# The last norm, residual and store, tile by tile inside the routed stage

## The chip, the cores and the metric

The kernel runs on one core of a Trainium2 chip. A core has five engines with instruction queues of their own: TensorE (PE, matrix products into PSUM), VectorE (DVE), ScalarE (ACT), GpSimd (POOL) and SyncE (SP, which here only issues DMAs). They work side by side and wait for one another through semaphores. The metric is the device time of one execution in microseconds. The kernel before takes 1456.02 us, the median of 3 runs (1454.44 to 1457.98).

## The reference

Input x is 8 sequences of 512 tokens with 256 features in float32. Two sublayers, each with a layer norm in front and one behind:

```
x = x + layernorm(mamba(layernorm(x)))
x = x + layernorm(ffn(layernorm(x)))
```

`mamba` is an input projection, a convolution over 4 tokens, a scan over 512 time steps with 16 states for each of 512 channels, and an output projection. `ffn` is a mixture of experts with one shared expert:

```
score  = sigmoid(max(x @ gate_w));  expert = argmax(x @ gate_w)       # 8 experts
routed = swiglu(x * score) with the weights of the token's one expert
shared = swiglu(x) with the shared weights
ffn    = shared + routed
```

A layer norm here is (v - mean) / sqrt(var + 1e-5) over the 256 features.

## The kernel before

**Scan stage.** The sequences go one after the other through a pipeline of 32 quarter steps each (`iteration`). Beside the scan the kernel writes to DRAM, for each sequence, the rows after the first sublayer (`x1_rows`, the later residual) and their normalized form (`xn_rows`, and transposed `xn_columns`). SP also fills `slot_in` with zeros once, early (line 418). The shared expert's result for sequence 0 is made within this stage.

**Shared stage.** TensorE runs the shared expert over the other 7 sequences. ScalarE copies the result out of PSUM into `ysh`, which stays in SBUF for all tokens (`sh_keep`, L908). Beside it VectorE works out the routing: each token gets a slot number so that the tokens of an expert stand together and each expert's slots fill whole tiles of 128; with 4096 tokens and 8 experts that makes 39 tiles, some slots empty. GpSimd multiplies the normalized rows by the score and scatters them to `slot_in` by indirect DMA, 32 tiles of 128 tokens (L574, L580). SP loads the expert weights.

**Routed stage.** Slot tiles s = 0 to 38, each of one expert. In `step(s)` TensorE issues: the transposes of the slot rows of tile s+2 (`xsT_`, L1632, into bank psB), the transposes of the activation of tile s (`actT_`, L1650), the gate and up projections of tile s+1 (`up_`, L1641), and the down projection of tile s (`down_`, L1658). VectorE copies xsT (L1264) and actT (L1276) out of PSUM and multiplies silu(gate) by up (`rt_act`, actN, L1270); ScalarE makes the silu (L949), copies the down projection out of PSUM (`rt_out`, L955) and stores it to `slot_out` (L957). SP reloads one of two slot buffers as soon as its transposes are made (L452). Each engine's order is written out by hand; these loops are loops of the machine (`Fori`), two tiles a round. GpSimd has nothing to do.

**Last stage.** It begins when all 39 tiles are stored. GpSimd gathers the routed rows back in token order, 32 indirect DMAs into a ring of eight pairs `fy` (L591). For each pair of token tiles VectorE adds `ysh` (`fin_sum`, L1302) and takes the statistics (L1305, L1310), ScalarE works out 1/sqrt by Ln and Exp and normalizes (`fin`, L980 to L991), VectorE adds the residual (`fin_out`, L1316; the residual rows were loaded into `fx0` and `fx1`), and SP stores to the result.

Of the kernel before, what the change touches and what calls it, by code (L numbers as in the profile page):

```python
# [7 lines left out]
F32 = mybir.dt.float32  # L8
# [5 lines left out]
P = 128  # L14
# [5 lines left out]
def build(nc, x, winT, conv_w, xprojT, dt_w, dt_b, A_log, D, woutT, norm_w, norm_b,  # L20
# [32 lines left out]
    FRING = 8  # L53
# [5 lines left out]
    xs_d = nc.dram_tensor("slot_in", (SLOT_TILES * P, DIM), F32).ap()  # L59
    y_d = nc.dram_tensor("slot_out", (SLOT_TILES * P, DIM), F32).ap()  # L60
    bc_d = nc.dram_tensor("bc_rows", (NB, 2 * N, L), F32).ap()
    ysh_d = nc.dram_tensor("shared_rows", (P, J, DIM), F32).ap()

    ctx = ExitStack()
    with ctx:
# [73 lines left out]

        fst = [sb(f"fst{i}", [P, 2, 6], where=M) for i in range(FRING)]  # L140
        fmv = [sb(f"fmv{i}", [P, 2, 2], where=M) for i in range(FRING)]
        fln = [sb(f"fln{i}", [P, 2], where=M) for i in range(FRING)]
        fnm = [sb(f"fnm{i}", [P, 2], where=M) for i in range(FRING)]
        frs = [sb(f"frs{i}", [P, 2], where=M) for i in range(FRING)]
        actT = [sb(f"actT{i}", [P, FC, P], where=M) for i in range(2)]
        yo = [sb(f"yo{i}", [P, DIM], where=M) for i in range(2)]
        sb("xg_rest", [P, 2 * KC * L - FRING * 22 - 2 * FC * P - 2 * DIM], where=M)
        WG = ExitStack()
        ctx.enter_context(WG)
        wg = sb("wg", [P, E, KC, FF], where=WG)  # L150
        WG.close()

        HALF = NT // 2
        fx1 = sb("fx1", [P, HALF, DIM], where=M)
        sb("wg_rest", [P, E * KC * FF - HALF * DIM], where=M)
        wu = sb("wu", [P, E, KC, FF], where=M)
        wd = sb("wd", [P, E, FC, DIM], where=M)
        fx0 = sb("fx0", [P, HALF, DIM], where=M)
        ysh = sb("ysh", [P, NT, DIM], where=M)
        sg = [sb(f"sg{i}", [P, FF], where=M) for i in range(2)]  # L160
        xsl = [sb(f"xsl{i}", [P, DIM], where=M) for i in range(2)]
# [7 lines left out]
        fy = [sb(f"fy{i}", [P, 2, DIM], where=M) for i in range(FRING)]  # L169
# [23 lines left out]
        xrow = [fx0[:, i * J:(i + 1) * J] for i in range(2)]  # L193
# [35 lines left out]
        ysh_loaded = sem("ysh_loaded")  # L229
# [77 lines left out]
        yo_ready = sem("yo_ready")  # L307
        yo_stored = [sem(f"yo_stored{i}") for i in range(2)]
        gathered = [sem(f"gathered{i}") for i in range(FRING)]
        f_loaded = [sem(f"f_half_loaded{i}") for i in range(2)]  # L310
        f_chain = sem("final_chain")
        f_normed = sem("final_normed")
        f_mv = sem("final_mv")
        f_rs = sem("final_rs")
        f_ready = sem("final_ready")
        f_stored = [sem(f"f_stored{i}") for i in range(2)]
# [5 lines left out]
        x1t_v = x1_d.rearrange("(t p) c -> p t c", p=P)  # L322
        xst_v = xs_d.rearrange("(t p) c -> t p c", p=P)
        yt_v = y_d.rearrange("(t p) c -> t p c", p=P)
        outp_v = out.rearrange("b (q h p) c -> (b q) p h c", p=P, h=2)
# [9 lines left out]
        def _(sp):  # L335
# [44 lines left out]
            def iteration(i, par, do_lead, do_front, do_scan, do_back):  # L380
# [8 lines left out]
                if do_back and not (do_scan or do_front):  # L389
                    sp.wait_ge(summed, NB * Q)  # L390
                    for k in range(2):
                        sp.dma_start(xrow[k], xnb_v[k]).then_inc(xrow_loaded[k], 16)
# [21 lines left out]
                if do_front:  # L414
# [5 lines left out]
                         ao[:, 0:1].broadcast_to([P, SLOT_TILES, DIM])).then_inc(slots_zeroed, 16)  # L420
# [10 lines left out]
            for i in range(2):  # L431
# [3 lines left out]
            sp.dma_start(ysh_d.rearrange("p j d -> p (j d)"),  # L435
                         tmp[:, 0:2].rearrange("p h t -> p (h t)")).then_inc(e_stored, 16)
# [13 lines left out]
            for b in range(2, NB):  # L450
                sp.wait_ge(scattered[b % 2], 16 * J * (b // 2))
                sp.dma_start(xrow[b % 2], xnb_v[b]).then_inc(xrow_loaded[b % 2], 16)  # L452
# [11 lines left out]
            def load_residual(dst, h):  # L464
                for g in range(NB // 2):
                    rows = slice((h * NB // 2 + g) * J, (h * NB // 2 + g + 1) * J)
                    sp.dma_start(dst[:, g * J:(g + 1) * J, :], x1t_v[:, rows, :]).then_inc(f_loaded[h], 16)

            sp.wait_ge(e_stored, 16)
            sp.dma_start(ysh[:, 0:J, :], ysh_d).then_inc(ysh_loaded, 16)  # L470
            load_residual(fx0, 0)
            with sp.Fori(0, SLOT_TILES - 4, 2) as s:
                for i in range(2):
                    sp.wait_ge(xsT_ready, s + i + 1)
                    load_slots(s + i + 2, i)
            for s in range(SLOT_TILES - 3, SLOT_TILES - 2):
                sp.wait_ge(xsT_ready, s + 1)
                load_slots(s + 2, s % 2)


            sp.wait_ge(r_up, SLOT_TILES)
            load_residual(fx1, 1)

            def store_out(q, i, src, first):
                sp.wait_ge(f_ready, q + 1)
                sp.dma_start(outp_v[bass.ds(q, 1)].rearrange("a p h c -> p (a h) c"),
                             src[:, bass.ds(2 * (q - first), 2), :]).then_inc(f_stored[i], 16)

            NQ = NT // 2
            for h, src in enumerate((fx0, fx1)):  # L490
                with sp.Fori(h * NQ // 2, (h + 1) * NQ // 2 - 1, 2) as q:
                    for i in range(2):
                        store_out(q + i, i, src, h * NQ // 2)
            sp.wait_ge(f_stored[0], 16 * (NQ // 2))
# [1240 lines left out]
```

## Time and profile before

| | us |
|---|---|
| median of 3 runs | 1456.02 |
| profiled execution, its time | 1456.55 |
| profiled execution, its span in the trace | 1454.6 |
| TensorE busy | 1180.4 (81%) |
| VectorE busy | 1029.7 (71%) |
| GpSimd busy | 997.9 (69%) |
| ScalarE busy | 801.9 (55%) |

The busy times are averages over stages with different limits: in the scan stage GpSimd and VectorE are busy almost throughout, in the shared and routed stages TensorE. The page also gives the granted clock of TensorE, in shares of full speed, and for each group of instructions the idle time of its engine just ahead of it with what ended that. Idle time of an engine that isn't the limit costs nothing. GpSimd's line L591 is an example of how to read this: it shows 286.6 us of idle time before it, 277.2 of them ended by the store of `slot_out`, which means only that GpSimd had no work during the routed stage.

### The profile page before, as it was taken

What the parts mean: (1) busy time and instruction counts of PE and PEld (TensorE: products, weight loads), DVE (VectorE), ACT (ScalarE), POOL (GpSimd) and SP (SyncE); (2) the same over time, 40 slices, a digit from 0 to 9 for tenths busy, and PEclk for the clock granted to TensorE, in tenths of its full rate; (3) what the DMA queues carried; (4) which work ended last, traced back from release to release, by engine and by line L of the source; (5) the groups of instructions that cost most, each with busy time, mean ns of one, the idle gap of its engine ahead of it and who ended that gap; (6) DMA issues with size and microseconds to landing.
All of it is one profiled execution on the core that took longest, in us unless ns stands there. A gap on an engine that the chain in (4) does not pass through costs nothing.

```text
span 1454.6 us, 15610 instructions
## 1 busy us (share of the span) xinstructions
PE 1180.4 (81%) x4782; PEld 521.0 (36%) x4783; DVE 1029.7 (71%) x1067; ACT 801.9 (55%) x1388; POOL 997.9 (69%) x468
## 2 busy tenths in 40 slices
PE   5667768878887896986987878889999999999930
PEld 2221223223222331421422322334566566666620
DVE  3598999999999989999999897993411122222237
ACT  5757458667677776875866865654411111111137
POOL 0589999999999999999999999993137000000035
PEclk9898899899899899999989999999999999999975
DMA  3901211230240250141122024002584211111145
GB/s 104 330 1 59 88 58 41 95 113 31 73 145 3 74 174 0 61 152 37 60 87 87 31 73 173 0 15 93 198 316 147 88 37 43 43 43 43 40 130 174
DMA packets 78246, 129.56 MB, mean 89 GB/s; under 512 B 7649, under 2 KB 56417, under 8 KB 74081
## 3 DMA queue, kind: packets, MB, share of 16 engines
q1 hardware_dynamic: 68768, 112.60, 23.1%
q0 software_dynamic: 3072, 8.39, 1.8%
q10 hardware_dynamic: 6336, 7.74, 1.5%
q8 instruction: 33, 0.54, 0.2%
q14 instruction: 37, 0.30, 0.1%
HBM read 96.46 MB, written 32.24 MB: 88 GB/s over the span
## 4 chain that ended last, share of the span: by engine, by line
PE 35%; POOL 33%; issue 15%; DVE 10%; ACT 6%; DMA 1%; POOLq 0%; ACTq 0%; SPq 0%; DVEq 0%
POOL state L528 20%; PE psX L1641 10%; POOL bx L517 10%; PE psX L1576 6%; DVE state L1111 6%; PE psY L1589 3%; PE bank L1658 2%; PE psY L1658 2%; POOL fy L591 2%; PE bank L1445 2%; POOL lt L533 2%; PE psY L1523 2%; ACT psX L754 1%; DVE bx L1099 1%; PE psY L1650 1%
## 5 line engine op out<-in xcount | busy, mean ns | idle before, releaser
L528 POOL TENSOR_TENSOR state<-state,cbc 128x1024 f32<-128x1024 f32 x256 | 605.6, 2388 | 16.1 <-DVE state L1111 16.0
L1111 DVE TENSOR_TENSOR_SCAN state<-psX,bx 128x1024 f32<-128x1024 f32 x256 | 578.5, 2279 | 38.7 <-ACT psX L754 22.3
L754 ACT ACTIVATE psX<-dt,aneg 128x511 f32<-128x511 f32 x512 | 330.6, 679 | 198.8 <-DVE state L1111 197.2
L517 POOL TENSOR_TENSOR bx<-xh,bbc 128x1024 f32<-128x1024 f32 x120 | 290.0, 2417 | 59.5 <-DMA bbc<-bc_rows 43.1
L1523 PE MATMUL psY<-state,ident 64*64 64x512 f32 x2048 | 288.0, 656 | 16.9 <-POOL state L528 16.8
L1480 PE MATMUL bank<-prow,ident 128*128 128x512 f32 x272 | 171.8, 717 | 112.9 <-DVE bx L1099 112.9
L591 POOL DMA_INDIRECT fy<-slot_out,slot x32 | 33.5, 1047 | 286.6 <-DMA slot_out<-yo 277.2
L1099 DVE TENSOR_TENSOR bx<-xh,bank 128x1024 f32<-128x1024 f32 x136 | 162.6, 1195 | 8.6 <-PE bank L1480 8.5
L1523 PEld LDWEIGHTS psY<-state,ident 64*64 64x64 f32 x2048 | 64.4, 140 | 202.7 <-issue 127.6
L1270 DVE TENSOR_TENSOR actN<-sg,psX 128x512 f32<-128x512 f32 x39 | 26.8, 687 | 141.1 <-ACT sg L949 141.1
L1480 PEld LDWEIGHTS bank<-prow,ident 128*128 128x128 f32 x272 | 48.5, 212 | 207.1 <-DVE bx L1099 166.7
L949 ACT ACTIVATE sg<-psX 128x512 f32<-128x512 f32 x39 | 23.3, 597 | 155.3 <-PE psX L1641 155.3
L1188 DVE TENSOR_TENSOR actS<-sg,psX 128x512 f32<-128x512 f32 x28 | 19.0, 685 | 102.8 <-ACT sg L902 102.8
L1641 PE MATMUL psX<-wg,xsT 128*128 x156 | 77.2, 617 | 1.1 <-DVE xsT L1264 0.6
L1641 PE MATMUL psX<-wu,xsT 128*128 x156 | 73.3, 592 | 0.0
L1400 PE MATMUL bank<-lt,win 128*128 128x512 f32 x112 | 55.6, 618 | 17.9 <-DVE acc L1046 16.5
L574 POOL TENSOR_TENSOR fx<-fx,score 128x1024 f32<-128x1024 f32 x8 | 15.3, 1911 | 74.0 <-DVE slot L1251 54.7
L1046 DVE SCALAR_TENSOR_TENSOR acc<-bank,cw,acc 128x511 f32<-128x511 f32 (+2 forms) x84 | 62.3, 741 | 3.9 <-ACT acc L645 1.9
L1445 PE MATMUL bank<-wout,yv 128*128 128x256 f32 x256 | 58.5, 382 | 1.7 <-ACT yv L700 1.6
L902 ACT ACTIVATE sg<-psX 128x512 f32<-128x512 f32 x28 | 16.6, 596 | 76.8 <-PE psX L1576 76.7
L1576 PE MATMUL psX<-xg,shg 128*128 128x512 f32 x112 | 53.1, 596 | 1.6 <-DVE actS L1188 1.6
L1445 PEld LDWEIGHTS bank<-wout,yv 128*128 128x128 f32 x256 | 48.0, 190 | 17.3 <-issue 9.0
(190 smaller groups left out, 1579.6 us busy)
## 6 DMA issues: line engine op xcount, KB each, us to landing
cbc<-bc_rows SPq DMA_DIRECT2D x32, 1024.0 KB, 5.0
bbc<-bc_rows SPq DMA_DIRECT2D x16, 1024.0 KB, 6.1
slot_in<-ao SPq DMA_DIRECT2D x1, 4992.0 KB, 27.9
xsl<-slot_in SPq DMA_DIRECT2D x39, 128.0 KB, 2.2
slot_out<-yo ACTq DMA_DIRECT2D x39, 128.0 KB, 2.4
xin<-in_x SPq DMA_DIRECT2D x8, 512.0 KB, 4.3
xr<-in_x SPq DMA_DIRECT2D x8, 512.0 KB, 5.4
x_rows<-ao SPq DMA_DIRECT2D x8, 512.0 KB, 2.9
```

Of the source, the lines that this page charges most:

```text
L517: nc.gpsimd.tensor_tensor(bx[q % RB][:], xh[par][:, h * CH:(h + 1) * CH], bbc[:, n // 2].unsqueeze(1).broadcast_to([P, CH, L]), ALU.mult). ...
L528: nc.gpsimd.tensor_tensor(w[:], w[:], cbc[:, n].unsqueeze(1).broadcast_to([P, CH, L]), ALU.mult).then_inc(weighted, 1)
L591: nc.gpsimd.indirect_dma_start(out=fy[q % FRING][:, t % 2, :], out_offset=None, in_=y_d, in_offset=bass.IndirectOffsetOnAxis(slot[:, t:t + ...
L754: e = nc.scalar.activation(decay[q % RD][:, c, 1:L], dt[par][:, h * CH + c, 1:L], ACT.Exp, scale=aneg[:, h * CH + c, n:n + 1])
L1046: last = nc.vector.scalar_tensor_tensor(out=acc[:, c, m:L], in0=psF[:, 0:L - m], scalar=cw[:, c, TAPS - 1 - m:TAPS - m], in1=acc[:, c, m:L ...
L1099: nc.vector.tensor_tensor(bx[q % RB][:], xh[par][:, h * CH:(h + 1) * CH], psB[:].unsqueeze(1).broadcast_to([P, CH, L]), ALU.mult).then_inc ...
L1111: nc.vector.tensor_tensor_scan(st[q % RS][:].rearrange("p c t -> p (c t)"), decay[q % RD].rearrange("p c t -> p (c t)"), bx[q % RB][:].rea ...
L1445: last = nc.tensor.matmul(psF[:, (j % 2) * DIM:(j % 2 + 1) * DIM], yv[:, c, j * P:(j + 1) * P], wout[:, c], start=(c == 0), stop=(c == C - 1))
L1480: nc.tensor.matmul(psB[:], ident[:, n:n + 1].broadcast_to([P, P]), prow[par][:], start=True, stop=True).then_inc(b_bcast, 1)
L1523: done = nc.tensor.matmul(psY[o * HP:(o + 1) * HP, r], weights(half, c), src[half, c], start=first, stop=last_)
L1576: last = nc.tensor.matmul(bank, w[:, k, c * P:(c + 1) * P], xg[g % 2][:, k], start=(k == 0), stop=(k == KC - 1))
L1641: last = nc.tensor.matmul(bank, xsT[i][:, k], w[:, bass.ds(ereg[i], 1), k].rearrange("p a n -> p (a n)"), start=(k == 0), stop=(k == KC - 1))
```

## The change

The token order is given up for the end of the kernel: each routed tile is finished where it stands. A slot row carries a 257th number, from which the token's number is read; empty slots carry 0, which gives 4096 and is out of bounds, so that the indirect DMAs leave such rows out. For tile s

- VectorE makes the index from the slot row (`token_index`);
- GpSimd gathers the shared rows (`ysl`, ring of 4) and the residual rows (`x1l`, ring of 8) of these tokens (`get`), and six tiles later scatters the finished tile to the result (`put`);
- VectorE adds the down projection, straight from PSUM, to the shared rows (`rt_sum`, one tile behind) and takes the statistics; for each pair of tiles it works out 1/sqrt with a bit trick and three Newton steps, in two halves (`root_begin`, `root_end`);
- ScalarE normalizes a pair (`rt_norm`), and VectorE adds the residual (`rt_add`).

The shared rows are therefore stored to DRAM, sequence by sequence, from ScalarE's queue. The loops of the routed stage on VectorE, ScalarE and GpSimd are now written out; TensorE's stay as they were. `slot_out`, the second table load, the residual loads and the old last stage are gone.

```diff
-    FRING = 8
+    YR = 8
+    SR = 4
+    IR = 16
+    PUT_LAG = 6
...
-    xs_d = nc.dram_tensor("slot_in", (SLOT_TILES * P, DIM), F32).ap()
-    y_d = nc.dram_tensor("slot_out", (SLOT_TILES * P, DIM), F32).ap()
+    xs_d = nc.dram_tensor("slot_in", (SLOT_TILES * P, DIM + 1), F32).ap()
...
@@ SP @@
                 for i in range(2):
                     sp.wait_ge(xsT_ready, s + i + 1)
+                    sp.wait_ge(idx_ready, s + i + 1)
                     load_slots(s + i + 2, i)
...
-            sp.wait_ge(r_up, SLOT_TILES)
-            load_residual(fx1, 1)
...
@@ GpSimd @@
+                nc.gpsimd.tensor_copy(xrow[b % 2][:, :, DIM:DIM + 1],
+                                      ids[:, b * J:(b + 1) * J].unsqueeze(2)).then_inc(xrow_scaled, 1)
...
+            def get(s):
+                pool.wait_ge(idx_ready, s + 1)
+                if s >= SR:
+                    pool.wait_ge(y_summed, s - SR + 1)
+                nc.gpsimd.indirect_dma_start(out=ysl[:, s % SR, :], out_offset=None, in_=ysh_d, in_offset=by_token(s),
+                                             bounds_check=TOK - 1, oob_is_err=False).then_inc(ysl_loaded[s % SR], 16)
+                if s >= YR:
+                    pool.wait_ge(o_ready, s - YR + 1)
+                nc.gpsimd.indirect_dma_start(out=x1l[:, s % YR, :], out_offset=None, in_=x1_d, in_offset=by_token(s),
+                                             bounds_check=TOK - 1, oob_is_err=False).then_inc(x1l_loaded[s % YR], 16)
+
+            def put(s):
+                pool.wait_ge(o_ready, s + 1)
+                nc.gpsimd.indirect_dma_start(out=out_v, out_offset=by_token(s), in_=yo[s % YR][:], in_offset=None,
+                                             bounds_check=TOK - 1, oob_is_err=False).then_inc(out_stored[s % YR], 16)
+
+            pool.wait_ge(s_down, 2 * LATE)
+            nc.gpsimd.memset(ysl[:], 0.0).then_inc(rings_zeroed, 1)
+            nc.gpsimd.memset(x1l[:], 0.0).then_inc(rings_zeroed, 1)
+            pool.wait_ge(rings_zeroed, 2)
+            pool.wait_ge(ysh_stored, 16 * LATE)
...
+            for s in range(SLOT_TILES + PUT_LAG):
+                if s < SLOT_TILES:
+                    get(s)
+                if s >= PUT_LAG:
+                    put(s - PUT_LAG)
@@ ScalarE @@
+                act.wait_ge(s_kept, 2 * g + 2)
+                act.dma_start(yshb_v[LATE_FROM + g],
+                              ysh[:, (LATE_FROM + g) * J:(LATE_FROM + g + 1) * J, :]).then_inc(ysh_stored, 16)
...
+            def rt_norm(k):
+                act.wait_ge(ln_ready, k + 1)
+                for s in range(2 * k, min(2 * k + 2, SLOT_TILES)):
+                    nc.scalar.activation(yo[s % YR][:], yo[s % YR][:], ACT.Identity,
+                                         scale=frs[k % 2][:, s % 2:s % 2 + 1],
+                                         bias=fnm[k % 2][:, s % 2:s % 2 + 1]).then_inc(y_normed, 1)
...
+            for s in range(SLOT_TILES):
+                rt_silu(s, s % 2)
+                if s >= 4 and s % 2 == 0:
+                    rt_norm(s // 2 - 2)
@@ VectorE @@
+            def rt_sum(s):
+                dve.wait_ge(r_down, s + 1)
+                dve.wait_ge(ysl_loaded[s % SR], 16 * (s // SR + 1))
+                if s >= YR:
+                    dve.wait_ge(out_stored[s % YR], 16 * (s // YR))
+                nc.vector.tensor_tensor(yo[s % YR][:], (psF, psG)[s % 2][:, 0:DIM], ysl[:, s % SR, :],
+                                        ALU.add).then_inc(y_summed, 1)
+                dve.wait_ge(y_summed, s + 1)
+                linked(nc.vector.bn_stats(out=fst[s % 2][:], in_=yo[s % YR][:]))
+                nc.vector.memset(carrier[:], 0.0)
+                linked(nc.vector.bn_aggr(out=fmv[s // 2 % 2][:, s % 2, :], in_=fst[s % 2][:]))
+
+            def newton(k, w):
+                y, v, q = part(frs, k, w), part(fvar, k, w), part(fsq, k, w)
+                linked(nc.vector.scalar_tensor_tensor(out=q, in0=y, scalar=-0.5, in1=y, op0=ALU.mult, op1=ALU.mult))
+                linked(nc.vector.tensor_tensor(q, q, v, ALU.mult))
+                linked(nc.vector.scalar_tensor_tensor(out=y, in0=q, scalar=1.5, in1=y, op0=ALU.add, op1=ALU.mult))
...
+            for s in range(SLOT_TILES):
+                if s + 2 < SLOT_TILES:
+                    copy_xsT(s + 2, s % 2)
+                    token_index(s + 2)
+                copy_actT(s, s % 2)
+                if s >= 1:
+                    rt_sum(s - 1)
+                if s % 2 == 0 and s >= 2:
+                    root_begin(s // 2 - 1)
+                if s % 2 == 1 and s >= 3:
+                    root_end(s // 2 - 1)
+                if s % 2 == 0 and s >= 4:
+                    rt_add(s - 4)
+                    rt_add(s - 3)
+                if s + 1 < SLOT_TILES:
+                    rt_act(s + 1, (s + 1) % 2)
+            T = SLOT_TILES
+            root_end(T // 2 - 1)
+            rt_sum(T - 1)
+            root_begin(T // 2, 1)
+            root_end(T // 2, 1)
+            for s in range(T - 3, T):
+                rt_add(s)
@@ TensorE, down_ @@
-                    pe.wait_ge(yo_ready, s - 1)
+                    pe.wait_ge(y_summed, s - 1)
```

`linked` adds one to a semaphore at an instruction's end and makes the next instruction of VectorE wait for it.

The next rows show VectorE in one round of the routed loop of the kernel before, two steps: xsT is the transposed slot rows, actT the transposed activation, actN the activation.

```order
L1264 COPY xsT<-bank 128x256
L1275 REGISTER_ALU
L1276 COPY actT<-psY 128x512
L1267 REGISTER_ALU
L1270 TENSOR_TENSOR actN<-sg,psX 128x512
L1261 REGISTER_ALU
L1264 COPY xsT<-bank 128x256
L1276 COPY actT<-psY 128x512
L1270 TENSOR_TENSOR actN<-sg,psX 128x512
```

In the changed kernel the same engine has this between the actT copy and actN of an even step (here s = 36; yo is the tile's row ring, ysl the shared rows, fvar to fsq the root's small tiles, x1l the residual rows):

```order
L1273 TENSOR_TENSOR yo<-psY,ysl 128x256
L1276 BN_STATS fst<-yo 128x6
L1277 MEMSET carrier 128x1
L1278 BN_AGGR fmv<-fst 128x2
L1291 TENSOR_SCALAR fvar<-fmv 128x2
L1292 TENSOR_SCALAR fbit<-fvar 128x2
L1293 TENSOR_SCALAR frs<-fbit 128x2
L1285 SCALAR_TENSOR_TENSOR fsq<-frs 128x2
L1286 TENSOR_TENSOR fsq<-fsq,fvar 128x2
L1287 SCALAR_TENSOR_TENSOR frs<-fsq,frs 128x2
L1306 TENSOR_TENSOR yo<-yo,x1l 128x256 x2
L1249 TENSOR_TENSOR actN<-sg,psX 128x512
```

Twelve instructions now stand between the copy and the multiplication that TensorE waits for, where there was none.

GpSimd before, from the last scatters of slot rows on (fx holds the scaled rows):

```order
L574 TENSOR_TENSOR fx<-fx,score 128x1024
L580 DMA slot_in<-fx,slot 4992x256 x4
L574 TENSOR_TENSOR fx<-fx,score 128x1024
L580 DMA slot_in<-fx,slot 4992x256 x4
L591 DMA fy<-slot_out,slot 128x256 x32
```

GpSimd in the changed kernel, the last two rounds of the routed stage (result is the output, x_rows the residual rows):

```order
L581 DMA ysl<-shared_rows,idx 128x256
L585 DMA x1l<-x_rows,idx 128x256
L590 DMA result<-yo,idx 4096x256
L581 DMA ysl<-shared_rows,idx 128x256
L585 DMA x1l<-x_rows,idx 128x256
L590 DMA result<-yo,idx 4096x256 x7
```

The 32 gathers in one run are gone; each tile has two gathers and a scatter, and seven scatters stand at the end.

## Rows read from the trace of the kernel before

**Rows 1.** windows view of two stretches: length, busy us by engine, PEclk, DMA share, GB/s
```profile
1157.00:1396.70 239.70, 236.54 (x854) 142.84 (x854) 69.37 (x115) 38.20 (x78) 0.00 (x0) 1.00 0.16 46
1396.70:1454.60 57.90, 0.00 (x0) 0.00 (x0) 36.16 (x112) 35.91 (x114) 33.50 (x32) 0.53 0.53 164
```

**Rows 2.** waits of the routed stage: engine, line waited for, us, times, longest
```profile
ACT sg L949 <- PE psX L1641: 155.3, 39, 5.3
```

**Rows 3.** chain that ended last, in order of time: start, us, what
```profile
1157.11 3.71 PE psX L1641 x8
...
1387.59 3.69 PE psX L1641 x8
...
1394.32 2.00 PE bank L1658 x8
...
1396.76 4.62 DMA slot_out<-yo
...
1440.70 4.03 DMA fy<-slot_out,slot
...
1451.09 0.69 DVE fx L1316
```

**Rows 4.** timeline of one routed step, all engines: start, us, engine, line, operation, idle before
```profile
1300.40 0.60 ACT L949 ACTIVATE sg<-psX 128x512 f32<-128x512 f32 x1 [4.00 <-PE psX L1641]
...
1301.03 0.69 DVE L1270 TENSOR_TENSOR actN<-sg,psX 128x512 f32<-128x512 f32 x1 [3.58 <-ACT sg L949]
...
1302.14 0.60 PE L1650 MATMUL psY<-ident,actN 128*128 128x128 f32 x4
...
1302.34 0.42 DVE L1264 COPY xsT<-bank 128x256 f32<-128x256 f32 x1 [0.63 <-PE bank L1632]
...
1302.78 0.69 DVE L1276 COPY actT<-psY 128x512 f32<-128x512 f32 x1
```

**Rows 5.** timeline of VectorE in the routing chain
```profile
1045.20 0.42 DVE L1238 TENSOR_TENSOR q<-bank,incl 128x256 f32<-128x256 f32 x1
...
1046.12 0.17 DVE L1242 TENSOR_SCALAR ti<-incl 128x8 int32<-128x8 f32 x1
...
1046.33 0.17 DVE L1243 TENSOR_SCALAR ti<-ti 128x8 int32<-128x8 int32 x1
```

**Rows 6.** the stretch after the routed stage, by line and form: busy us, mean ns
```profile
L591 POOL DMA_INDIRECT fy<-slot_out,slot x32 | 33.5, 1047 | 286.6 <-DMA slot_out<-yo 277.2 <-issue 9.4
...
L991 ACT ACTIVATE fy<-fy,fnm,frs 128x256 f32<-128x256 f32 x32 | 17.5, 592 | 0.5
...
L1305 DVE BATCH_NORM_STATS2 fst<-fy 128x6 f32<-128x256 f32 x32 | 12.0, 418 | 0.5
...
L1310 DVE BATCH_NORM_AGGREGATE fmv<-fst 128x2 f32<-128x6 f32 x32 | 3.9, 163 | 0.7
```

**Rows 7.** timelines of GpSimd and VectorE in the last stage
```profile
1418.34 1.35 POOL L591 DMA_INDIRECT fy<-slot_out,slot  x1 [0.31 <-issue]
...
1419.07 0.69 DVE L1302 TENSOR_TENSOR fy<-fy,ysh 128x512 f32<-128x512 f32 x1 [0.21 <-DMA fy<-slot_out,slot]
```

**Rows 8.** end of the scatter on GpSimd and of the shared stage
```profile
1123.49 0.96 POOL L580 DMA_INDIRECT slot_in<-fx,slot  x1 [0.30 <-issue]
...
1155.06 0.38 PE L1632 MATMUL bank<-ident,xsl 128*128 128x128 f32 x2
...
1155.26 0.60 ACT L908 ACTIVATE ysh<-psY 128x512 f32<-128x512 f32 x1 [2.86 <-PE psY L1589]
```

**Rows 9.** DMA issues of the whole program: KB each, median us to landing
```profile
slot_in<-ao SPq DMA_DIRECT2D x1, 4992.0 KB, 27.9
...
slot_in<-fx,slot POOLq DMA_INDIRECT x32, 3.5
```

**Rows 10.** start of the program, timelines of the SP queue and of GpSimd
```profile
41.58 0.57 SPq L419 DMA_DIRECT2D slot_in<-ao  x1
...
107.06 4.68 POOL L528 TENSOR_TENSOR state<-state,cbc 128x1024 f32<-128x1024 f32 x2
```

## What is predicted

> **What bounds the kernel now.** I read the windows first, to cut the span where the kernel's stages end, then the chain that ended last, then the waits and one step's timeline. The routed stage (39 tiles of 128 slots) is TensorE's: it is busy 236.54 of 239.70 us at granted clock 1.00, that is 2.4 GHz, while VectorE is busy 69 us and GpSimd not at all; in the 57.90 us behind it TensorE does nothing [rows 1]. ScalarE's silu waits 155.3 us for TensorE there, 39 times [rows 2]. The chain gives the pace: from the first tile's up-projection at 1157.11 to the last one's at 1387.59 are 38 steps, 6.065 us each. The last down-projection ends at 1396.32. Then a store has to land, all 32 gathers go through GpSimd one behind the other, and the last add runs from 1451.09 to 1451.78 [rows 3]; the span ends at 1454.60, 2.82 us later, with the last store. So 58.3 us stand behind TensorE's end, and the change can win at most these. It can lose wherever a step comes to need more than 6.065 us.
>
> **The slack in a step.** In one step [rows 4] silu ends, VectorE multiplies (actN) from 1301.03 to 1301.72, and TensorE's four transposes of it start at 1302.14: actN could be about 0.4 us later before TensorE waits. The copy of these transposes (actT) runs from 1302.78 to 1303.47, and VectorE then idles 3.58 us until the next actN. The window for new work between copy and actN is thus 3.58 + 0.4 = 3.98 us. Into it go, for every tile, the sum with the shared part and its statistics, and by turns the first or the second half of the root and the two residual adds.
>
> **Prices on VectorE.** The sum (128x256, one operand in PSUM): 0.42 [rows 5]. Statistics 0.42, aggregate 0.16 [rows 6], the small memset in its shadow. Each instruction that waits for its forerunner starts about 0.04 late: the two dependent 128x8 instructions start 0.21 apart with 0.17 of work [rows 5]. So sum and statistics are 0.46 + 0.46 + 0.20 = 1.12 us. A link of the root's chain (128x2) is taken as 0.21. The trace shows no such Newton step; it is bounded by 0.17 without a wait and by 0.46, what a dependent 128x256 instruction takes; I take 0.21, the row nearest in size. The residual add is 0.42, from the sum's row again; a 128x512 add is 0.69 [rows 7], so it lies between 0.35 and 0.69.
>
> Even step: 1.12 + 6 links 1.26 + 2 adds 0.84 = 3.22 us. The token index (128x1, 0.17 or less) stands ahead of the actT copy and delays it by at most 0.1, since the copy would start only 0.02 after the xsT copy. 3.22 + 0.1 against 3.98 leaves 0.66 us. Odd step: 1.12 + 7 links 1.47 = 2.59, leaving 1.3. I cost the whole new VectorE work of the stage at nothing: TensorE's up-projection and silu cover it. If the cover is gone, each of the 17 even steps with adds (s = 4 to 36) pays its overrun in full. With both bounds put in, an even step is 1.12 + 1.02 + 0.70 = 2.84 or 1.12 + 2.76 + 1.38 = 5.26: from nothing to an overrun of 1.4 us, or 24 us in all.
>
> **ScalarE.** The two normalizations of a pair (0.59 each, rows 6) follow an even step's silu, which ends 1301.00 in rows 4, so they end about 1.2 us later and the adds that wait for them come 4 us later; the next silu is 6 us off. The copy out of PSUM and 39 stores leave ScalarE, and TensorE's down-projection waits for VectorE's sum two tiles back, a step before it. Nothing.
>
> **GpSimd and the queues.** Three indirect DMAs per tile. In the last stage one takes 1.047 on average and 0.30 between two [rows 6, 7], the longest shown 1.35 + 0.31. Three are 4.0 us, at worst 5.0, of 6.065. The gather of shared rows for tile s may be issued in step s-2, and its sum stands in step s+1; residual rows have longer, and a scatter is six tiles behind its gather. What queues behind a waiting scatter are the next gathers, which have two steps to spare. The bound check on the index, and the rows that it drops, are in no row: from below such a DMA is as short as an undisturbed one, 0.96 [rows 8]; from above I put GpSimd's 128x1024 multiply, 4.68 / 2 = 2.34 [rows 10], and three of these are 7.0 a tile, 0.95 over the step or 36 us in all. I take the gather's own row, nothing lost, and leave the upper end to a rival.
>
> The stage's start: the last shared rows are copied at 1155.86 [rows 8]. Two memsets of 3072 columns are less than three such multiplies, 7.0 us, so the gathers start between 1159 and 1163, and the first sum is due after the actT copy of tile 1, two steps behind 1157.11, near 1170; a landing takes 3.5 us [rows 9]. Covered.
>
> Ahead of the stage: the seven 512 KB stores and eight tiny copies lie beside the shared stage. GpSimd's scatter ends 1124.45 and the first slot transpose is at 1155.06 [rows 8], 30 us of cover. SP's slot loads now also wait for the index, about 0.5 us later, with a whole step of slack; SP loses the residual loads. The slot fill, now 1028 bytes a row, goes out at 41.58 and lands 27.9 later [rows 9, 10], at 69.5. The C rows queued behind it are read from 107 on, so it may even double. Nothing.
>
> **The new tail**, from the old clock. TensorE ends at 1396.32. VectorE has had the last actT copy at 1394.2: sum of tile 37 to 1395.4, first half of root 18 to 1396.6, two adds to 1397.5, second half to 1398.9, sum of tile 38 to 1400.1, both halves of root 19 (13 links) to 1402.8, with the normalization of tile 38 to 1403.5 and its add to 1403.9. Tiles 36 and 37 are added from 1402.8 on; GpSimd scatters three tiles from 1403.3, the third at 1403.3 + 2 x 1.27 = 1405.8 (1.27 where it is undisturbed, 0.96 + 0.30, rows 8), landing 3.5 later at 1409.3 [rows 9], and about 0.5 to the end of the span, my share of the 2.82 above, which hold a store's landing and the end. Span 1409.8. Gain: 58.3 - 13.5 = 44.8 us. The profiled execution took 1456.55 for its span of 1454.60, 1.95 more, and lies 0.53 above the median of 1456.02. 1409.8 + 1.95 - 0.53 = 1411.2 us, so 1411.
>
> **Rivals.**
> *The window overruns* (0.14). An instruction with two or three waits may cost more than the 0.04 seen. For it: eleven of the even step's twelve instructions behind the copy wait, and the spare is 0.66 us. Against it: the dependent instructions of the routing chain keep 0.21. With 0.1 more for eleven it pays (1.1 - 0.66) x 17 = 7 us; with the upper bound 24. I take 13, toward the middle: 1424.
>
> *The shared port* (0.11). In rows 7 a GpSimd DMA runs from 1418.34 to 1419.69 and a VectorE add with both operands in SBUF starts at 1419.07 inside it and takes its plain 0.69, so VectorE isn't held; GpSimd's DMA is 0.4 longer than the undisturbed. If VectorE were held for the DMAs that fall into its window, an even window of 3.2 us would meet 6 x 3.2 / 12.13 = 1.6 of them, 1.5 us, 0.8 over the spare, in 17 steps 14 us: 1425. The Trainium skill speaks against this change here: "SBUF — State Buffer", section "Who interferes with whom", has VectorE and GpSimd share one port pair as an exclusive lock, for which a VectorE instruction with two SBUF inputs or in a two-port mode contends, and the later one blocks. By that rule the time is 1425; the trace agrees for GpSimd's side alone.
>
> *GpSimd becomes the bound* (0.09), the one that ends on the other side. Mechanism: a bound-checked indirect DMA costs more than the gather in the rows, or small VectorE instructions hold it up. From 2.02 us each (6.065 / 3) it sets the pace of the routed stage; from 2.02 + 44.8 / 114 = 2.41 us the kernel is slower than before. At 2.5 it is 7.5 x 38 - 230.5 = +54 us: 1466. For it: 117 of them inside the stage, where before there was none, and the price of the bound check is unknown. Against: 1.66 is the longest distance seen with VectorE as busy.
>
> *Early work isn't covered* (0.06): the 1028-byte rows triple the fill, or the weight and slot traffic delays the first tile: some 9 us, 1420.
>
> **How the numbers follow.** Forecast 1411 with 0.60; its own range is 1405 to 1418 (tail links at 0.17, scatters landing in 3; or a first step late by some us). A difference under 0.2% (3 us) can't be told from none. Of GpSimd's 0.09, 0.06 end slower, 0.01 the same and 0.02 faster. So faster 0.93, same 0.01, slower 0.06. The range runs from 1405 to 1432: it takes in the window and port cases but for the last of their upper bound, and leaves out GpSimd's.
>
> **What would show it.** Right: TensorE's step stays 6.07 at clock 1.00; VectorE's idle time before actN is 0.3 to 0.5 in even steps and near 1 in odd ones; 117 indirect DMAs near 1.0 to 1.35; some 13.5 us from TensorE's end to the span's end. Wrong: TensorE's transposes waiting for actN, with even steps longer than odd ones (window, or port, if the wait falls on GpSimd's DMAs); sums waiting for shared rows and GpSimd without idle time (GpSimd bound); a first tile later than 1157 (early work).

## The result, and the profile after

The changed kernel takes 1411.37 us (median of 4 runs, 1410.87 to 1412.14), the kernel before 1455.23 beside it (1454.25 to 1457.98): a ratio of 0.9699, 95% interval 0.968 to 0.9718. Forecast were 1411. The profiled execution took 1411.09 us for a span of 1409.3.

The same two stretches as in [rows 1], in the windows view of the changed kernel:

```profile
1157.00:1396.70 239.70, 236.49 (x854) 142.59 (x853) 159.53 (x579) 40.88 (x75) 115.36 (x113) 1.00 0.25 75
1396.70:1409.30 12.60, 0.00 (x0) 0.00 (x0) 5.64 (x29) 1.69 (x3) 4.92 (x5) 0.60 0.02 2
```

TensorE's stage is as it was, to 0.05 us, and at the same clock (1.00, that is 2.4 GHz). VectorE does 90 us more beside it and GpSimd 115 us where it did nothing, and the stretch behind has shrunk from 57.90 to 12.60 us. The chain that ended last, in order of time, against [rows 3]:

```profile
1156.74 3.71 PE psX L1647 x8
...
1387.59 3.69 PE psX L1647 x8
...
1394.09 0.42 DVE yo L1273
...
1402.25 0.84 DVE yo L1306 x2
...
1405.72 0.98 POOL result L590
```

38 steps from 1156.74 to 1387.59 are 6.075 us each (6.065 before). Where the old chain went on with a store, gathers and a last add at 1451, it now leaves TensorE for VectorE's sums, roots and adds, and ends with a scatter on GpSimd. TensorE's last product ends at 1396.31, and 13.0 us stand behind it, where the forecast had 13.5. Who waits in the routed stage (engine, line waited for, us, times, longest), against [rows 2]:

```profile
ACT sg L961 <- PE psX L1647: 196.5, 39, 5.6
POOL ysl L581 <- DVE idx L1258: 75.9, 36, 3.9
...
DVE actN L1249 <- ACT sg L961: 41.6, 38, 4.5
...
PE psY L1656 <- DVE actN L1249: 1.2, 1, 1.2
```

GpSimd waits 76 us for token indices: it has time. TensorE's transposes wait for an actN once (1.2 us); in the kernel before this wait is there too (1.3 us, once). One even step with its adds, from the timeline, against [rows 4]:

```profile
1294.75 0.69 DVE L1249 TENSOR_TENSOR actN<-sg,psX 128x512 f32<-128x512 f32 x1 [1.17 <-ACT sg L961]
...
1296.50 0.69 DVE L1255 COPY actT<-psY 128x512 f32<-128x512 f32 x1
1297.11 0.42 DVE L1273 TENSOR_TENSOR yo<-psY,ysl 128x256 f32<-128x256 f32 x1
...
1298.66 1.01 POOL L585 DMA_INDIRECT x1l<-x_rows,idx  x1 [0.31 <-issue]
1298.90 0.16 DVE L1285 SCALAR_TENSOR_TENSOR fsq<-frs 128x2 f32<-128x2 f32 x1
1299.09 0.16 DVE L1286 TENSOR_TENSOR fsq<-fsq,fvar 128x2 f32<-128x2 f32 x1
...
1299.48 0.76 DVE L1306 TENSOR_TENSOR yo<-yo,x1l 128x256 f32<-128x256 f32 x2
1300.20 0.60 ACT L961 ACTIVATE sg<-psX 128x512 f32<-128x512 f32 x1 [4.51 <-PE psX L1647]
...
1300.84 0.69 DVE L1249 TENSOR_TENSOR actN<-sg,psX 128x512 f32<-128x512 f32 x1 [0.59 <-ACT sg L961]
```

Links of the root's chain start 0.19 to 0.20 apart. The new work, sum to last add, runs from 1297.11 to 1300.24, 3.13 us. VectorE then idles 0.59 us before actN in this even step and 1.17 in the odd one (the first row). GpSimd's DMAs in the same stretch, by line and form, against [rows 6]:

```profile
L581 POOL DMA_INDIRECT ysl<-shared_rows,idx x39 | 40.3, 1033 | 80.6 <-DVE idx L1258 75.9 <-issue 4.7
L585 POOL DMA_INDIRECT x1l<-x_rows,idx x39 | 39.2, 1006 | 11.9 <-issue 11.9
...
L590 POOL DMA_INDIRECT result<-yo,idx x34 | 35.2, 1036 | 23.3 <-DVE yo L1306 18.1 <-issue 5.2
```

They take 1.01 to 1.04 us with the bound check, where the unchecked gathers took 1.047. And the issues of the whole program, against [rows 9]:

```profile
slot_in<-ao SPq DMA_DIRECT2D x1, 5011.5 KB, 35.1
...
result<-yo,idx POOLq DMA_INDIRECT x39, 2.5
```

Last the end, in the timeline:

```profile
1397.64 0.98 POOL L590 DMA_INDIRECT result<-yo,idx  x1 [9.39 <-DVE yo L1306]
...
1398.46 1.09 ACT L966 ACTIVATE yo<-yo,fnm,frs 128x256 f32<-128x256 f32 x2 [5.57 <-DVE fnm L1300]
...
1400.38 0.99 POOL L590 DMA_INDIRECT result<-yo,idx  x1 [1.76 <-issue]
...
1401.91 1.17 DVE L1306 TENSOR_TENSOR yo<-yo,x1l 128x256 f32<-128x256 f32 x3
...
1403.14 0.98 POOL L590 DMA_INDIRECT result<-yo,idx  x1 [1.77 <-DVE yo L1306]
...
1405.72 0.98 POOL L590 DMA_INDIRECT result<-yo,idx  x1 [0.30 <-issue]
```

The rows of tiles 36 and 37 are normalized by 1399.55 and wait for their add until 1401.91, behind the root of tile 38. From the last scatter's start to the end are 3.6 us. What they hold is seen only at the line to which the engines' closing drains are put down (operation, duration ns, start):

```profile
L68 POOLq DRAIN  x1: 5050/5050/5050, 1404.0 to 1404.0; - x1
...
L68 SPq DRAIN  x1: 13/13/13, 1408.1 to 1408.1; - x1
```

SP, which waits for all scatters to land, is done at 1408.1; GpSimd's drain runs to 1409.07, and this is what ends the program. Its record begins at 1404.0, before the last two scatters, so its 5.05 us cover these and their landing as well; 0.9 us of it stands behind SP.

### The profile page after: what moved, and what is told of

Read it like the earlier page. It is cut to its first block, busy times and chain, and to the rows that moved or that the text cites. A ratio compares the mean times of both kernels' runs of the same rounds, so it can differ in the third digit from the quotient of the medians.

```text
span 1409.3 us, 15754 instructions
## 1 busy us (share of the span) xinstructions
PE 1175.4 (83%) x4782; PEld 518.5 (37%) x4783; DVE 1089.8 (77%) x1449; ACT 770.9 (55%) x1275; POOL 1088.4 (77%) x565
## 4 chain that ended last, share of the span: by engine, by line
PE 36%; POOL 29%; issue 15%; DVE 12%; ACT 8%; DMA 0%; POOLq 0%; ACTq 0%; SPq 0%; DVEq 0%
POOL state L511 18%; PE psX L1647 10%; POOL bx L500 9%; DVE state L1090 6%; PE psX L1582 5%; PE psY L1595 3%; PE psY L1664 2%; PE bank L1664 2%; PE psY L1529 2%; PE bank L1451 2%; POOL lt L516 2%; ACT psX L763 2%; PE bank L1486 1%; DVE bx L1078 1%; DVE acc L1025 1%
## 5 line engine op out<-in xcount | busy, mean ns | idle before, releaser
L581 POOL DMA_INDIRECT ysl<-shared_rows,idx x39 | 40.3, 1033 | 80.6 <-DVE idx L1258 75.9
L1406 PE MATMUL bank<-lt,win 128*128 128x512 f32 x112 | 55.5, 618 | 15.7 <-DVE acc L1025 14.4
L590 POOL DMA_INDIRECT result<-yo,idx x39 | 40.1, 1029 | 36.8 <-DVE yo L1306 29.3
L1249 DVE TENSOR_TENSOR actN<-sg,psX 128x512 f32<-128x512 f32 x39 | 26.8, 688 | 44.1 <-ACT sg L961 41.6
## 6 DMA issues: line engine op xcount, KB each, us to landing
slot_in<-ao SPq DMA_DIRECT2D x1, 5011.5 KB, 35.1
```

## The experiments

All of them change the changed kernel, but for one, and keep its computation unless it is said. The kernel before took 1455.2 to 1456.1 us beside them, and 1464.6 beside the three runs told of where they stand.

**Is VectorE's window as wide as I took it?** Added links in every even step that has adds, ahead of actN (a product of 128x2 whose result nobody reads):

```diff
...
                     rt_add(s - 4)
                     rt_add(s - 3)
+                    if s + 1 < SLOT_TILES:
+                        for _ in range(4):
+                            linked(nc.vector.tensor_tensor(fdum[:], fvar[0][:], fvar[0][:], ALU.mult))
```

> Four more dependent 128x2 multiplications on VectorE in each of the 17 even steps that have residual adds, between the adds and actN (their result isn't used). In the changed kernel's trace a link takes 0.195 us, so 0.78 us more per even step. Theory W (the window): VectorE idles 0.59 us before actN in such a step, and actN may be 0.4 us late before TensorE's transposes wait, so 0.95 us are to spare; nothing is paid: 1411 us. Rival F (no slack behind actN: what delays it is paid in full): 0.78 - 0.55 = 0.2 us in 17 steps, 1415 us.

> Eight such links in each of the 17 even steps, 1.56 us more. Theory W: 0.6 us over the spare of 0.95 us, paid 17 times, 10 us: 1422 us, with TensorE's transposes waiting for actN in even steps alone. Rival F: 1.0 us in 17 steps, 1428 us. If VectorE's delay were caught up again in the odd steps, which have 1.2 us idle, it would be 1411 us.

Measured: four links 1413.35 us (1412.55 to 1414.46; ratio 0.9715, 0.9684 to 0.9746), eight 1427.46 (1426.42 to 1429.47; 0.9817, 0.9786 to 0.9849). With four, actN starts 0.1 to 0.2 us behind silu's end in most of these steps (0.03 in the changed kernel), and the stage is 2.3 us longer (38 steps in 233.19 instead of 230.85, 0.14 for each of the 17 even ones), so even that little isn't absorbed. With eight, actN starts 0.91 to 0.97 us behind silu's end in most of them, and the 38 steps take 246.54 us, 15.7 more, or 0.92 for each even one: TensorE pays all of it. The 0.4 us between actN and the transposes were no slack. TensorE's waits with eight links, and its timeline, say why:

```profile
PE psY L1660 <- DVE actN L1250: 7.5, 17, 1.2
PE psX L1651 <- issue: 5.0, 16, 0.3
```

```profile
1296.12 0.69 DVE L1250 TENSOR_TENSOR actN<-sg,psX 128x512 f32<-128x512 f32 x1
...
1296.87 0.66 PE L1660 MATMUL psY<-ident,actN 128*128 128x128 f32 x4 [0.35 <-DVE actN L1250]
...
1297.82 1.98 PE L1651 MATMUL psX<-wg,xsT 128*128 x4 [0.30 <-issue]
```

The wait for actN is 0.35 to 0.4 a time, as the 0.4 of slack would have it; but then TensorE loses another 0.3 waiting for nothing that the profile shows, and starts its next product 0.95 us after the transposes instead of 0.62. At line 1676 of this kernel, just behind the wait for actN, its sequencer reads the next tile's expert number: a load of 0.30 us and about 0.2 of register work. With the order turned round:

```diff
...
                 if ahead:
                     xsT_(s + 2, i)
+                if more:
+                    expert(s + 1, 1 - i)
                 actT_(s, i)
                 if more:
-                    expert(s + 1, 1 - i)
                     up_(s + 1, 1 - i)
```

> The eight added links of the run before, and one thing moved: TensorE's sequencer reads the number of the next tile's expert (a load of 0.30 us, then 0.15 and 0.02 us of register work) ahead of its wait for actN, not behind it. In the run with eight links actN is ready 0.91 us late in every even step, and the step is 0.87 longer; the first matmul of the next product starts 0.95 us after the transposes of actN, against 0.62 in the changed kernel, with 0.3 us put down to issue (17 times, 5.3 us in all). Theory R (the lost 0.3 us is the sequencer's: its load waits behind the late actN, and only there): with the load ahead of the wait the first matmul starts 0.62 to 0.7 after the transposes, an even step is 6.6 to 6.65, the stage gives back 17 x 0.3 = 5 us, and the time is 1422 to 1423. Rival X (it is VectorE's: the copy of xsT stands behind the late actN and comes late too): nothing moves, even steps stay at 6.94, 1427.

Measured: 1417.26 us (1417.0 to 1419.29), beside a kernel before of 1464.59 (ratio 0.9679, 0.9664 to 0.9694). The times of two chips are hard to set against each other, so I go by the profiles: 38 steps take 235.81 us (first product at 1159.74, last at 1395.55) instead of 246.54. The load was the lost time, but it was worth 10.7 us, twice what I expected of it, since it was not paid in the late steps alone. With the load first, from the timelines of VectorE and TensorE, a late actN and one that isn't late; then TensorE in an undisturbed step of the changed kernel:

```profile
1294.07 0.69 DVE L1250 TENSOR_TENSOR actN<-sg,psX 128x512 f32<-128x512 f32 x1
...
1295.30 1.88 PE L1651 MATMUL psX<-wg,xsT 128*128 x4
...
1299.57 0.69 DVE L1250 TENSOR_TENSOR actN<-sg,psX 128x512 f32<-128x512 f32 x1 [0.94 <-ACT sg L962]
...
1300.68 0.60 PE L1660 MATMUL psY<-ident,actN 128*128 128x128 f32 x4
...
1301.12 1.88 PE L1651 MATMUL psX<-wg,xsT 128*128 x4
...
1302.84 1.88 PE L1651 MATMUL psX<-wu,xsT 128*128 x4
```

```profile
1295.87 0.60 PE L1656 MATMUL psY<-ident,actN 128*128 128x128 f32 x4
...
1296.47 1.98 PE L1647 MATMUL psX<-wg,xsT 128*128 x4
...
1298.29 1.88 PE L1647 MATMUL psX<-wu,xsT 128*128 x4
```

From transposes to product 0.44 instead of 0.60, and the product's first half 1.72 instead of 1.82: about 0.26 us in every step. The pace of 6.07 us that I had taken for TensorE's own work, in both kernels, has the sequencer's load in it.

The distance from the end of actN to TensorE's next product says it most plainly. With the load behind the wait it is 1.03 us where actN isn't late (1295.44 to 1296.47 in the changed kernel) and 1.01 where it is late by 0.9 (1296.81 to 1297.82), so all lateness is passed on. With the load first it is 0.86 where actN isn't late (1300.26 to 1301.12) and 0.54 where it is (1294.76 to 1295.30): 0.3 us of lateness is absorbed, and the slack that I had read is there once nothing of the sequencer stands behind the wait.

How the changed kernel does with the load first and no added links wasn't run; 38 x 0.26 is 9.9 us, as an estimate, if VectorE's even steps (0.59 us idle) follow.

**How near is GpSimd to being the bound?** One and three more gathers per tile, of shared rows into a ring that nobody reads:

```diff
...
+                if s < SLOT_TILES:
+                    for j in range(3):
+                        more(3 * s + j)
```

> One more gather of 128 shared rows per tile on GpSimd, into a spare ring that nothing reads, 39 more in all: four indirect DMAs per tile. Theory G (GpSimd's cost is its issue time, 1.03 + 0.30 us each, beside everything): 4 x 1.33 = 5.3 us of a step's 6.07, nothing is paid: 1411 us. Rival P (GpSimd's DMAs hold up VectorE through a shared port): one more in every step, up to 1 us in the even step's window against a spare of 0.95 us: 1411 to 1415 us, with VectorE's instructions longer or later in the window.

> Three more gathers per tile, six indirect DMAs in all. Theory G: 6 x 1.33 = 8.0 us per tile, 1.9 over the step of 6.07 in 38 steps: about 1411 + 73 = 1484 us, slower than the kernel before, with GpSimd without idle time in the routed stage and the sums waiting for it. Rival: if the DMAs' issue overlaps (the 0.30 us between them vanishes when they are queued, or one waits only for its descriptors), 6 x 1.0 = 6.0 and the time stays near 1411.

Measured: one more, 1415.15 us (1414.76 to 1415.65; ratio 0.9727, 0.9697 to 0.9757); three more, 1482.24 (1479.48 to 1483.3; 1.0185, 1.0151 to 1.0219). One more leaves the step at 6.073 us and VectorE's idle time before actN at 42.3 us (41.6 in the changed kernel), so the 4 us that it costs aren't the port rival's; 3.6 of them stand behind TensorE's end (see the next experiment). Three more make GpSimd the bound, as my third rival had it, and the kernel slower than before. In VectorE's waits, 1160 to 1450, and in GpSimd's timeline:

```profile
DVE yo L1287 <- DMA ysl<-shared_rows,idx: 82.4, 29, 3.4
```

```profile
1384.29 1.01 POOL L585 DMA_INDIRECT ysl<-shared_rows,idx  x1 [0.30 <-issue]
...
1392.24 1.01 POOL L585 DMA_INDIRECT ysl<-shared_rows,idx  x1 [0.30 <-issue]
```

Six DMAs take 7.95 us, 1.325 each with the 0.30 between them, and the sums wait for shared rows. The changed kernel's three take 3.97 of 6.075.

**Do GpSimd's DMAs hold VectorE up?** Both gathers left out, so that zeros are added for the shared part and for the residual:

```diff
...
-                if s < SLOT_TILES:
-                    get(s)
...
```

> Leaves out both gathers of each tile (78 indirect DMAs): the shared and residual rows added are zeros from the rings' memset. The scatters stay. Theory W/G (TensorE sets the pace, GpSimd's DMAs are hidden and hold nobody up): 1411 us within 0.2%, VectorE's instructions in an even step as long as in the changed kernel. Rival P (the DMAs hold VectorE up through a shared port, hidden by its spare): time 1411 us too, but VectorE's idle time before actN in even steps grows from 0.59 us by a good part of a DMA's 1.03 us. Rival D (traffic or late rows cost the step's pace its last hundredth, 6.075 against 6.065 us): 0.4 us less.

Measured: 1415.54 us (1414.3 to 1416.39; ratio 0.9723, 0.9707 to 0.9739), not faster at all. The step stays at 6.07 us, and VectorE's idle time before actN is what it was (41.6 with the gathers):

```profile
DVE actN L1248 <- ACT sg L960: 42.8, 38, 4.5
```

So the gathers cost VectorE about 1 us over 39 tiles, and TensorE nothing. The span of this profile is 5.3 us longer than the changed kernel's. TensorE's first product began 2.1 us later, already behind a slower scan; the stage was 0.3 shorter; and 3.5 are at the other end, as in the run with one gather more. There GpSimd's closing drain is 3.4 to 3.6 us longer:

```profile
L68 POOLq DRAIN  x1: 8445/8445/8445, 1405.9 to 1405.9; - x1
...
L68 SPq DRAIN  x1: 13/13/13, 1409.9 to 1409.9; - x1
```

SP has seen everything land by 1409.9, and the span ends at 1414.6. With one gather more the two numbers are 8.64 us and 1409.0. The record of a drain can begin before the last scatters, so its length isn't a price; the time from the last scatter's start to the end of the span is. That is 3.58 us, to 0.01, in the changed kernel (both times), with links, with extra fills and with either other tail, nine profiles in all, and 7.1 and 7.2 in these two and 9.5 with three more gathers. In just these three there is no pause between the first two scatters of the end (0.30 us), where each of the nine has one of 1.75 or 1.76. What joins the two stays open; it isn't the number of DMAs, since one of the two has more and one fewer.

**What would halving the old gathers have given?** The kernel before with 16 of its 32 gathers (the other rows are zeros):

```diff
...
-            for t in range(NT):
+            for t in range(0, NT, 2):
...
```

> The kernel before, with only the first of each pair's two gathers (16 instead of 32; the other half of each pair is zero rows plus the shared rows). It asks what bound the old last stage. Theory G (GpSimd's 32 DMAs, 1.35 us apart, 43 of its 58 us): with one per pair the next limit is ScalarE's chain of about 2.3 us per pair, 16 x 2.3 = 36 after the first: the stage gets about 5 to 8 us shorter, 1448 to 1451 us. Rival (a gather's bandwidth or landing bound it, or ScalarE and VectorE did already): no change, 1455 us. If GpSimd alone had bound it, it would fall by 21 us to 1434.

Measured: 1447.45 us (1439.1 to 1447.81; ratio 0.993, 0.9904 to 0.9957), 8.7 us less. GpSimd was the old tail's bound by that much only: behind it ScalarE and VectorE are busy 34.6 and 34.9 of the 48.9 us left, and GpSimd's last gathers each wait 1.10 us for VectorE. The 44 us came from putting the whole tail beside TensorE, not from cheaper gathers.

**Is the slot fill free, and why is it slower?** First the fill three times over, and the scatter made to wait for all:

> The zero fill of the slot rows is made three times (two of them into spare tensors, ahead of the real one): some 35 us each. The prediction gave it cover until the C rows behind it are read at 107 us: three fills end near 42 + 105 = 147. Theory C (cover to 107, then paid in full, as the queue is in order): 107 to about 147, some 30 to 45 us lost: 1441 to 1456. Rival (the later loads share the engines and aren't behind the fill, or the scan has slack of its own): 1411 to 1420.

Measured: 1430.18 us (1424.4 to 1431.19; ratio 0.9829, 0.9812 to 0.9845), between the two expectations; the wait is another one (VectorE, 30 to 170 us):

```profile
DVE bst L1009 <- DMA xin<-in_x: 18.5, 1, 18.5
```

Not the C rows are late but the next block's input tile, issued behind the fills. In the changed kernel it lands at 78.3 and is first read at 98.98, 20.7 us of room. That is what is left after the fill had grown by 7.2: in the kernel before the tile lands at 70.8 and is read from 98.4 on, 27.6 us of room. So "may even double" (27.9 more) named about the whole of it, though from another limit, the C rows at 107. Two more fills move the tile's landing by 37 us and not by 70: they overlap, and the three land at 74.2, 93.6 and 114.4. Then four extra fills of one size, well apart, in iterations 1 to 4, that differ in the floats of a row and the distance between rows:

```diff
+    FORMS = ((257, 257), (257, 320), (256, 256), (256, 257))
```

> Four more fills of 4992 rows into spare tensors, one behind each of the iterations 1 to 4, from a constant tile: rows of 1028 bytes at a pitch of 1028; 1028 at 1280; 1024 at 1024; 1024 at 1028. It asks why the slot fill went from 27.9 to 35.1 us. Only the time from issue to landing of each counts; the whole time is longer. Theory A (the start's alignment in DRAM costs it): slow, fast, fast, slow, near 35 and 28. Theory L (the length, one more piece of 4 bytes): slow, slow, fast, fast. Both: the second and fourth between.

Measured: 1412.28 us (one run), and landings of 27.6, 23.6, 21.0 and 28.0 us, in this order. Rows of 257 floats at a distance of 320 take 2.6 more than the plain form, either kind of row at a distance of 257 about 7 more. That is the size of the 7.2 us between [rows 9] and 35.1. With one measurement for each form, it is mainly the distance between the rows that costs (the second and fourth forms tell it from the length); why, and how much of the 2.6 is the longer row, isn't shown.

**Can the end be shorter?** The adds of tiles 36 and 37 ahead of the last root; and, in a second kernel, two Newton steps in place of three besides:

```diff
...
+            rt_add(T - 3)
+            rt_add(T - 2)
             root_begin(T // 2, 1)
             root_end(T // 2, 1)
-            for s in range(T - 3, T):
-                rt_add(s)
+            rt_add(T - 1)
```

> The changed kernel with the last adds of tiles 36 and 37 ahead of the last root and not behind it. In the changed kernel their rows are ready (ScalarE's norm ends 1399.55) 2.4 us before they are added (1401.91). Now they are added from 1399.5 to 1400.35, root 19 and its norm come 0.84 later, its add ends at 1403.9 against 1403.08, and by 0.8 us from the end of an add to its scatter (1402.34 to 1403.14) the last scatter starts at 1404.7 against 1405.72, where it stood third in a row of 1.29 each. Theory Q (the end is set by three scatters in a row behind one add): the end is 1.0 us earlier, 1410.4. Rival Z (GpSimd's pause of 1.76 us between two scatters comes again, or the three scatters still meet): 1411.0 to 1411.7, no change.

> As the run with the last adds moved, and with two Newton steps for each root and not three (less exact, by design): three links less in every odd step and in each of the two roots of the end. In the stage nothing changes (odd steps already have time to spare: TensorE's step stays 6.07). At the end the links are on the path: root 18 and root 19 are 3 x 0.195 = 0.58 us shorter each, so that the last add is 1.17 us earlier. Theory Q: 1410.4 - 1.2 = 1409.2. Rival Z: scatters of 36 and 37 hold the last one back (each takes 1.29): 1410.0 or more.

Measured, beside a kernel before of 1464.59: 1410.0 us (1408.89 to 1411.96; ratio 0.963, 0.9617 to 0.9643) and 1409.72 (1408.4 to 1411.57; 0.9631, 0.9618 to 0.9644). To have the changed kernel's own spread beside them:

> The changed kernel itself, unaltered, once more, since the two runs with another tail were timed on a chip on which the kernel before took 1464.6 us, and the changed kernel's own 1411.4 stands beside 1455.2. Theory Q (the tail runs gained what their profiles show behind TensorE's end: 11.8 and 11.5 us against 13.0): the changed kernel takes 1411 to 1412, 1.2 to 1.7 us more than they did, and 13.0 us stand behind TensorE's end again. Rival: the chips differ by more than that for this kernel too, in which case its time is outside 1410.5 to 1412.5 and the gain of the tail runs can be read from their profiles alone.

Measured: 1412.43 us (1410.95 to 1413.08), but beside 1455.27 (ratio 0.9702, 0.9689 to 0.9716), so on another chip again. The ratios can't be compared, and by the times the gain of 1.4 to 2.7 us is about what can be told. The profiles have it from the start of TensorE's last product: the changed kernel ends 14.98 us later (the same when run again), with the adds moved 13.81, with two Newton steps as well 13.49. The first gain is 1.2 us, where 1.0 was expected; of the second, 1.2 expected, only 0.3 came. The timeline with both:

```profile
1399.38 0.98 POOL L590 DMA_INDIRECT result<-yo,idx  x1 [1.76 <-DVE yo L1305]
...
1401.21 0.43 DVE L1305 TENSOR_TENSOR yo<-yo,x1l 128x256 f32<-128x256 f32 x1 [0.67 <-ACT yo L966]
1401.94 0.98 POOL L590 DMA_INDIRECT result<-yo,idx  x1 [0.30 <-DVE yo L1305]
1403.23 0.98 POOL L590 DMA_INDIRECT result<-yo,idx  x1 [0.30 <-issue]
```

The last add is done at 1401.64 and its scatter starts at 1403.23, behind the one before it: the pause of 1.76 us ahead of it in this row of scatters, which is in the changed kernel as well, leaves no room for the rest. In all of these kernels the span ends 3.58 us behind the last scatter's start.

## Why the prediction was right, and where it wasn't

**The step.** Right: 6.075 us at clock 1.00, VectorE's idle time 0.59 and 1.17 (forecast 0.3 to 0.5 and near 1), the new work hidden. Links cost 0.195 instead of 0.21, and the even step 3.13 instead of 3.22. The step of the argument that failed is "actN could be about 0.4 us later before TensorE waits": the runs with added links show that TensorE pays for a lateness of less than 0.2 already (2.3 us over the stage), since a load of its sequencer stands behind the wait; with the load moved ahead of it, 0.3 us is absorbed. The spare was the 0.59 us of idle time and no more. For an even step heavier by 0.6 to 1.0 us the same reasoning would have forecast no loss, and been wrong.

**GpSimd.** Right: 3.97 us a tile, the bound check costs nothing that shows (1.01 to 1.04 us against 1.047), and at twice the number it is the bound, slower than before.

**The port.** The rival is refuted, by the run without gathers. The residual adds have both operands in SBUF; the pair at 1299.48 begins inside a GpSimd DMA (1298.66 to 1299.67) and takes 0.38 an add. All that the trace shows is some 0.04 us on a small instruction under which a DMA starts: the root's third link takes 0.213 us (median of 18), and 0.169 in the run without gathers, where none starts there. The Trainium skill's rule ("SBUF — State Buffer", section "Who interferes with whom"), as I applied it in the prediction, would have held these adds up, and the trace disagrees. I had left out a line of the same section: two inputs in SBUF contend with a GpSimd instruction that reads SBUF, and it infers that a tensor_tensor doesn't stall the issue of DMAs. With that the trace agrees: the adds take their 0.38 us inside a DMA.

**Early work.** Right that it is covered; the fill was mis-sized, 35.1 us for 27.9. What it must not delay is the next input tile at 98.98, not the C rows at 107; behind the longer fill 20.7 us of room are left. The scatter of slots ended at 1128.55, 4.1 later than before, and was covered.

**The end.** The steps hold: scatters forecast from 1403.3 and the third at 1405.8, measured 1403.14 and 1405.72. The last term, landing and end, was put at 4.0 us and measured 3.6, but it is another one than I named: these scatters land in 2.1, and GpSimd's drain ends the program. A size nearly right, with a cause that was wrong; in three of the runs the term is 3.5 to 5.9 us longer. The span came out 0.5 below the forecast of 1409.8, and the median lies 2.1 above the profiled span where I had 1.4. That 1411.37 was measured for 1411 is luck to this extent: the two misses cancel, and TensorE's first routed product alone starts anywhere from 1155.7 to 1159.7 in profiles whose code is the same up to there.

## What to carry to other kernels

When an engine is the bound, look at what its sequencer does between the instructions as well: a pace that repeats exactly can hold a fixed load that no busy time shows, and what looks like slack in front of a wait may be used up behind it. A stage that follows the bound engine is worth its whole length if it can be cut by tiles, once every other engine's work per tile is summed against the pace; halving its slowest part gave 9 us here, moving the whole 44. Behind such a move, the end is a chain of single instructions, and it pays to walk it in order: what stands ready and waits behind work that doesn't need it.

## What the hardware showed that I had not expected

- A register load on TensorE's sequencer (0.30 us, and 0.2 of register work) behind a wait costs 0.26 us in every step, though TensorE is shown busy 236.5 of 239.7 us.
- GpSimd's closing drain ended the program, 0.9 us behind the moment when SP had seen every scatter land (1409.07 and 1408.1), and 4.3 to 6.6 us behind it in three other kernels.
- GpSimd paused 1.75 or 1.76 us between the first two scatters of the end in nine profiles, and all nine end 3.58 us behind the last scatter's start; the three without the pause end 7.1 to 9.5 us behind it.
- A broadcast store to DRAM rows 257 floats apart landed in 27.6 and 28.0 us, to rows 256 apart in 21.0 (one DMA of each form).
